# A routed feed-forward on one core: 71 blocks instead of 72, and the last batch finished in two halves

## The chip, the cores and the metric

The kernel runs on one core of a Trainium2 chip. The metric is the device time of one execution in microseconds (us); less is better. Before the change the median of three runs is 690.12 us.

## The reference

One layer of a transformer on x of shape (8, 512, 128), that is 8 batches of 512 rows, all in float32:

```
x = layernorm(x + attention(x))          # 16 heads of 8
gates = sigmoid(x @ Wg)                  # 8 experts, the best 2 of each row, weights normalised to 1
shared = silu(x @ Ws1) * (x @ Ws3) @ Ws2
routed = sum over the 2 experts e of w_e * (silu(x @ We1[e]) * (x @ We3[e])) @ We2[e]
out = layernorm(x + (shared + routed) / 3)
```

## The kernel before, in words

The kernel has an attention part (up to about 530 us) and a feed-forward part. Each of the five engines runs its own hand-written order of instructions; semaphores (`need`, `wait_ge`, `then_inc`) join them.

**Blocks.** While attention runs, each row of x is scattered twice into `slots_dram`, once for each expert it chose, so that every block of 128 slots belongs to one expert. 4096 rows times 2 give 8192 entries, 64 full blocks; each of 8 experts can leave a block open, so the kernel computes `SLOTS` = 72 blocks, in `G` = 9 groups k of `NBUF` = 8 (r = 0 to 7). Slots that no row fills hold a blank row whose result is dropped.

**One block.** For block n = 8k + r, SP loads the 128 slots (`moe_sync.block`, L1270). TensorE turns them (L1559), multiplies them with the expert's first weights in three products (L1579 to L1581), turns the gated result (L1589) and multiplies with the second weights (L1601). ScalarE applies silu (L1470) and scales the result (L1477); VectorE multiplies (L1418) and copies (L1414). GpSimd scatters the 128 results with an indirect DMA to `y2_dram` (L1242), where each row of x has two places. The engines take one block after another in `run_blocks`, which runs G + 4 = 13 groups; in the last four no blocks are left, and `exists` skips their steps.

**The end of a batch.** Blocks of group k hold rows of batches up to k, so batch n is complete when group n + 1 has been scattered. `ended(g, 3)` is the batch whose pairs SP loads at the end of group k (`load_pairs`, L1259: 512 KB, two rows of results for each row of x) after it has waited for the scatters (`y_stored`). VectorE then adds the pair (`add_pair`, L1363), adds the shared part and x (`add_sum`, L1370), takes statistics (`final_statistics`, L1376) and aggregates them (`final_mean`, L1384), for each of the four tiles of 128 rows, and forms variance and negated mean of all four (L1388, L1389). In steady work these steps are spread over the blocks of a group. One group later (`ended(g, 4)`) GpSimd raises the variance to the power -1/2 and multiplies (`final_deviation`, L1227 and L1229, at r = 0 ahead of the group's scatters), ScalarE normalises four tiles (`final_normalize`, L1452) and issues the store of 256 KB to the output (`store_out`, L1457).

**Order at the end.** In GpSimd's program the deviation of batch 5 stands after the scatters of group 8 (blocks 64 to 71), followed by those of batches 6 and 7. The sums z have two buffers, so batch 7 may be added only when batch 5's store has landed:

```
if c == 0:
    need(dve, yb_loaded[slot], 16 * (uses + 1))
    need(dve, out_stored[slot], 16 * uses)
```

VectorE's last rows take batch 7 tile by tile; in these lists `prob` is the large tile in which all buffers of this part lie.

Of the kernel before, what the change touches and what calls it, by code (L numbers as in the profile page):

```python
# [41 lines left out]
ALU = mybir.AluOpType  # L42
# [3 lines left out]
P = 128  # L46
EPS = 1e-5
TOP_K = 2
# [62 lines left out]
def layer(nc, x, w_qkv, b_qkv, w_out, b_out, wg, ws1, ws3, ws2, we1, we3, we2, out):  # L111
    B, S, D = x.shape
    E, _, F = we1.shape
    NC = 16
    HD = D // NC
    NCH = S // P
    QUADS = B * S // P
    TILES = QUADS
# [9 lines left out]
    ROW = D + 2  # L128
    NFC = F // P
    NBUF = 8  # L130
    assert SLOTS % NBUF == 0 and SLOTS % 8 == 0
    jobs = Jobs(B)
    SETUP_STEPS = 4
    CLEARS = 7
# [3 lines left out]
    with ctx:  # L138
# [6 lines left out]
        def sem(name):  # L145
            return ctx.enter_context(nc.semaphore(name))
# [983 lines left out]
        y_stored = [sem(f"y_stored{n}") for n in range(NBUF)]  # L1130

        yb_loaded = [sem(f"yb_loaded{r}") for r in range(2)]
        pair_done = sem("pair_done")
        z_done = sem("z_done")
        fstats_done = sem("fstats_done")
# [26 lines left out]
        AHEAD = 3  # L1162

        def vector_count(n, copied, multiplied, turned):

            return AHEAD + 3 * n - min(n, 2) - max(n - (SLOTS - AHEAD), 0) + (n >= 2 and copied) + multiplied \
                + (n < SLOTS - AHEAD and turned)

        def y_ebT_count(n):

# [1 line left out]

        def copied_count(n):

            return vector_count(n + 2, True, False, False) if n + 2 < SLOTS else \
                vector_count(SLOTS - 1, True, True, True) + n + 2 - (SLOTS - 1)

        def gated_count(n):

# [4 lines left out]
            return n + 1 if n < AHEAD else vector_count(n - AHEAD, True, True, True)  # L1184

        def exists(k, r, back=0):
            return not isinstance(k, int) or 0 <= NBUF * k + r - back < SLOTS


        hT = scoreA[:].rearrange("p a b x -> p (a b) x")  # L1190
# [20 lines left out]
        def moe_gpsimd(pool):  # L1211
            pool.wait_ge(pv_done, QUADS)
            pool.iota(block_no_i[:], pattern=[[0, 1]], base=0, channel_multiplier=1).then_inc(late_const, 1)
            pool.memset(turn[:], 1.0).then_inc(late_const, 1)
            pool.wait_ge(late_const, 2)
            pool.tensor_copy(block_no[:], block_no_i[:]).then_inc(late_const, 1)
            pool.memset(turn[:, :, E - 1:E], float(1 - E)).then_inc(late_const, 1)
            deviation(pool, B)
            scatter_rows(pool, B - 2, range(NCH * TOP_K))
            copy_rows(pool, B - 1)  # L1220
            scatter_rows(pool, B - 1, range(NCH * TOP_K))

            def final_deviation(n):

                need(pool, fve_done, 2 * (n + 1))
                need(pool, norm_done, 4 * n)
                pool.tensor_tensor(frs[:], fve[:], half[:], ALU.pow).then_inc(frs_done, 1)  # L1227
                need(pool, frs_done, n + 1)
                pool.tensor_tensor(fmr[:], fneg[:], frs[:], ALU.mult).then_inc(fmr_done, 1)  # L1229

            def block(g, r):
                k = g.k
                n = NBUF * k + r
                if r == 0 and ended(g, 4):
                    final_deviation(ended(g, 4).n)
                if not exists(k, r):
                    return

                at = NBUF * g.odd + r
                need(pool, block_loaded[at], 16 * (g.m + 1))  # L1240
                need(pool, y_done, n + 1)
                pool.indirect_dma_start(y2_dram, bass.IndirectOffsetOnAxis(ap=eb[:, at, D:D + 1].bitcast(I32), axis=0),  # L1242
                                        yo[:, r, :], None, bounds_check=TOP_K * TILES * P, oob_is_err=False) \
                    .then_inc(y_stored[r], 16)

            run_blocks(pool, block)

        def moe_sync(sp):

            store_x1(sp, B)  # L1250
            sp.wait_ge(x1_stored, 64 * B)
            load_x1(sp, B - 1)

            sp.wait_ge(scattered, CLEARED + 16 * TILES * TOP_K)

            def load_pairs(batch):

                need(sp, pair_done, 4 * (batch.n - 1))
                sp.dma_start(yb[:, batch.slot].rearrange("p c j d -> p (c j d)"),  # L1259
                             y2_rows[batch.n] if isinstance(batch.n, int) else  # L1260
                             y2_rows[bass.ds(batch.n, 1)].rearrange("b p x -> (b p) x")).then_inc(yb_loaded[batch.slot], 16)
# [12 lines left out]

            run_blocks(sp, block)
            for slot in range(2):
                sp.wait_ge(out_stored[slot], 16 * (B // 2))

        def moe_vector(dve):
            def beside(n):  # L1280
# [97 lines left out]
            def final_mean(batch, c):  # L1378
# [5 lines left out]
                dve.bn_aggr(fmv[:, c, :], fst[:, c, :]).then_inc(fmv_done, 1)  # L1384
                if c == 3:
                    dve.wait_ge(fmv_done, 4 * n + 4)
                    need(dve, fmr_done, n)
                    dve.tensor_scalar(fve[:], fmv[:, :, 1], EPS, None, ALU.add).then_inc(fve_done, 1)  # L1388
                    dve.tensor_scalar(fneg[:], fmv[:, :, 0], -1.0, None, ALU.mult).then_inc(fve_done, 1)  # L1389

            def beside_block(g, r):
                before_last, this = ended(g, 4), ended(g, 3)
# [30 lines left out]

            run_blocks(dve, block)

        def moe_scalar(act):
            for n in range(STEPS):
                b, c = n // 4, n % 4
# [17 lines left out]
            for n in range(3):  # L1446
                ebT_round(n, n)

            def final_normalize(batch, c):
                need(act, fmr_done, batch.n + 1)  # L1450
# [12 lines left out]
            def block(g, r):  # L1463
                k = g.k
                n = NBUF * k + r
                if exists(k, r):
                    act.wait_ge(h_gT_ready, n + 1)
                    if n >= 2:
                        act.wait_ge(vector_done, gated_count(n - 2))
                    act.activation(silu[:, r % 2, :], h_bank(r)[:, 0:F], ACT.Silu).then_inc(silu_done, 1)  # L1470
                if exists(k, r, 4):
                    c = (r - 4) % NBUF
                    at = NBUF * ((g.odd + (r - 4) // NBUF) % 2) + c
                    act.wait_ge(y_ebT_ready, y_ebT_count(n))
# [6 lines left out]
                if ended(g, 4):  # L1481
                    for c in NORMALIZED_AT.get(r, ()):
                        final_normalize(ended(g, 4), c)
                    if r == NBUF - 1:
                        store_out(ended(g, 4))

            run_blocks(act, block)

        def moe_tensor(pe):

# [76 lines left out]
            def block(g, r):  # L1567
# [23 lines left out]
                if n < SLOTS + 2:  # L1591
# [68 lines left out]
```

## Time and profile before

| | |
|---|---|
| median of three runs | 690.12 us (687.95 to 690.82) |
| the profiled execution, its own time | 686.2 us |
| its span | 684.5 us |
| TensorE (PE) busy | 640.4 us, 94% |
| VectorE (DVE) busy | 548.9 us, 80% |
| ScalarE (ACT) busy | 424.2 us, 62% |
| GpSimd (POOL) busy | 269.4 us, 39% |
| mean granted TensorE clock | 0.98 of full speed |

The span runs from the first to the last instruction of the profile; the execution's own time is 1.7 us longer. The profile names lines of the kernel and tiles; PE is TensorE's matmuls, PEld its weight loads, SPq and ACTq are the queues on which SP and ScalarE issue DMAs. Idle time of an engine matters only if the engine is on the chain of work that ends last.

### The profile page before, as it was taken

The numbers are of one execution on the slowest core, as the hardware profiler recorded it, in microseconds if no ns is written. First come the engines' busy times: TensorE is split into PE (matmuls) and PEld (weight loads), VectorE is DVE, ScalarE is ACT, GpSimd is POOL, SyncE is SP. The second block draws the span as 40 slices with busy tenths as digits, with TensorE's granted clock in tenths as the row PEclk, the third lists the DMA queues.
The fourth block names the chain that finished last, engine by engine and source line by source line (L and its number), as shares of the span: only waits on it lengthen the run. The fifth ranks groups of instructions, "written<-read, shape, count | busy, mean of one in ns | idle before, by whom it ended". The sixth has DMA issues, their size and how long they took to land.

```text
span 684.5 us, 16202 instructions
## 1 busy us (share of the span) xinstructions
PE 640.4 (94%) x4653; PEld 320.8 (47%) x4653; DVE 548.9 (80%) x1272; ACT 424.2 (62%) x973; POOL 269.4 (39%) x402
## 2 busy tenths in 40 slices
PE   8899999999999999999999999999899989999970
PEld 5442333333334333333343334333258878888760
DVE  4895677779897997998899799797667767888882
ACT  2065677776676776677767667766734346666752
POOL 3322112333144335314434432540525526677772
PEclk9998899999999999999999999999999999999995
DMA  4557466344433324442333342330132033444522
GB/s 84 122 122 175 100 137 156 82 88 105 74 84 79 84 50 78 96 89 62 85 72 64 89 101 53 66 89 15 52 108 63 32 83 88 146 141 132 164 74 77
DMA packets 161857, 62.68 MB, mean 92 GB/s; under 512 B 110586, under 2 KB 155516, under 8 KB 161808
## 3 DMA queue, kind: packets, MB, share of 16 engines
q1 hardware_dynamic: 155008, 46.72, 31.2%
q0 software_dynamic: 5648, 13.26, 6.4%
q10 hardware_dynamic: 1152, 2.10, 0.8%
q8 instruction: 24, 0.39, 0.2%
q14 instruction: 25, 0.20, 0.1%
HBM read 38.04 MB, written 24.26 MB: 91 GB/s over the span
## 4 chain that ended last, share of the span: by engine, by line
PE 64%; issue 11%; POOL 8%; DVE 7%; DMA 4%; ACT 4%; SPq 2%; POOLq 0%; ACTq 0%; DVEq 0%
PE pvp L1051 16%; PE scoreB L1026 15%; PE scoreA L1012 14%; POOL y_dram L1242 6%; DVE mx L946 4%; DMA parts_dram<-parts 3%; ACT prob L919 2%; PE shared L534 2%; PE scoreB L1527 2%; PE shared L523 2%; PE pvp L995 1%; PE shared L518 1%; PE shared L553 1%; POOL prob L1227 1%; PE shared L542 1%
## 5 line engine op out<-in xcount | busy, mean ns | idle before, releaser
L919 ACT ACTIVATE prob<-scoreB 128x512 f32<-128x512 f32 x512 | 278.7, 600 | 125.9 <-PE scoreB L1026 125.5
L946 DVE TENSOR_REDUCE mx<-scoreA 128x2 f32<-128x1024 f32 x256 | 304.5, 1219 | 65.1 <-PE scoreA L1012 62.5
L1026 PE MATMUL scoreB<-qs,ks 74*128 74x512 bf16 x512 | 197.0, 387 | 6.4 <-ACT prob L919 3.0
L1012 PE MATMUL scoreA<-ks,qs 72*128 72x512 bf16 x512 | 195.2, 386 | 4.7 <-DMA ks<-parts_dram 2.4
L1051 PE MATMUL pvp<-prob,v 128*32 128x512 f32 x1024 | 137.6, 611 | 0.8 <-ACT pv_sb L911 0.8
L1012 PEld LDWEIGHTS scoreA<-ks,qs 72*128 72x128 bf16 x512 | 49.6, 99 | 138.9 <-DVE mx L946 65.1
L1026 PEld LDWEIGHTS scoreB<-qs,ks 74*128 74x128 bf16 x512 | 49.3, 97 | 100.3 <-ACT prob L919 77.6
L1242 POOL DMA_INDIRECT y_dram<-prob x72 | 70.8, 983 | 44.2 <-issue 30.7
L497 POOL DMA_INDIRECT slots_dram<-rows,slot_i x64 | 63.3, 990 | 56.5 <-DMA ks<-parts_dram 31.4
L846 POOL CAST parts<-qk 128x256 bf16<-128x256 f32 x32 | 12.7, 396 | 180.9 <-ACT v_raw L572 169.6
L1601 PE MATMUL scoreB<-w,prob 128*128 x288 | 44.2, 276 | 1.1 <-DVE prob L1414 1.1
L1470 ACT ACTIVATE prob<-scoreA 128x256 f32<-128x256 f32 x72 | 27.6, 383 | 22.4 <-PE pvp L1589 10.7
L1601 PEld LDWEIGHTS scoreB<-w,prob 128*128 128x128 f32 x288 | 37.8, 191 | 1.5 <-issue 1.3
L1579 PE MATMUL scoreA<-w_high,ebT_high 128*128 x72 | 34.5, 480 | 3.5 <-DVE gated L1418 3.5
L1418 DVE TENSOR_TENSOR gated<-scoreA,prob 128x256 f32<-128x256 f32 x72 | 30.2, 420 | 7.9 <-ACT prob L1470 7.4
L1051 PEld LDWEIGHTS pvp<-prob,v 128*32 128x32 f32 x1024 | 20.4, 108 | 29.4 <-issue 27.8
L1477 ACT ACTIVATE prob<-scoreB,prob 128x128 f32<-128x128 f32 x72 | 26.6, 369 | 11.7 <-PE scoreA L1559 9.3
L568 ACT ACTIVATE qk<-shared,bq 128x128 f32<-128x128 f32 x64 | 20.0, 363 | 18.7 <-PE shared L523 11.1
L645 POOL TENSOR_SCALAR veps<-mv 128x4 f32<-128x4 f32 x8 | 1.8, 227 | 73.2 <-DVE mv L627 73.2
L1348 DVE TENSOR_TENSOR ebT_low<-scoreA,ebT_high 128x128 fp32r<-128x128 f32 x72 | 20.8, 290 | 10.4 <-ACT ebT_high L1444 8.6
L1581 PE MATMUL scoreA<-w_high,ebT_low 128*128 x72 | 28.4, 395 | 0.0
L1580 PE MATMUL scoreA<-w_low,ebT_high 128*128 x72 | 28.3, 394 | 0.0
(178 smaller groups left out, 921.0 us busy)
## 6 DMA issues: line engine op xcount, KB each, us to landing
qs<-parts_dram SPq DMA_DIRECT2D x96, 96.0 KB
parts_dram<-parts SPq DMA_DIRECT2D x32, 192.0 KB
slots_dram<-blank POOLq DMA_DIRECT2D x9, 520.0 KB, 7.2
prob<-slots_dram SPq DMA_DIRECT2D x72, 65.0 KB, 1.9
ks<-parts_dram SPq DMA_DIRECT2D x64, 64.0 KB
prob<-y_dram SPq DMA_DIRECT2D x8, 512.0 KB, 3.3
ks<-parts_dram SPq DMA_DIRECT2D x32, 96.0 KB
xin<-in_L_attn_x SPq DMA_DIRECT2D x32, 64.0 KB, 2.2
```

Source lines behind the costliest of these rows:

```text
L497: pool.indirect_dma_start(slots_dram, bass.IndirectOffsetOnAxis(ap=slot_i[:, j, t:t + 1], axis=0), rows[:, t, j, :], None).then_inc(scatte ...
L919: act.activation(prob[:, i % 2, j, 2 * u + c, :], scoreB[:, c], ACT.Exp, scale=SCALE).then_inc(exp_done, 1)
L946: dve.tensor_reduce(mx[:, i % 2, at // 2, at % 2 * 2:at % 2 * 2 + 2], scoreA[:, at % 2], AX.X, ALU.max).then_inc(max_done, 1)
L1012: ins = pe.matmul(scoreA[:, at % 2, c], qs[0:KR, st, j, qc * P:(qc + 1) * P], ks[0:KR, st, j, :], start=True, stop=True)
L1026: pe.matmul(scoreB[:, c], ks[0:KM, i, j, kc * P:(kc + 1) * P], qs[0:KM, i, j, :], start=True, stop=True).then_inc(b_ready, 1)
L1051: ins = pe.matmul(pvp[32 * h:32 * h + 32, :], v[:, (i - 1) % 2, h, j, :], prob[:, (i - 1) % 2, h, j, :], start=(j == 0), stop=(j == 3))
L1242: pool.indirect_dma_start(y2_dram, bass.IndirectOffsetOnAxis(ap=eb[:, at, D:D + 1].bitcast(I32), axis=0), yo[:, r, :], None, bounds_check= ...
L1418: dve.tensor_tensor(gated[:, r % 4, :], h_bank(r)[:, F:2 * F], silu[:, r % 2, :], ALU.mult) \
L1579: pe.matmul(h, ebT_highs[:, r % 4], high, start=True, stop=False)
L1580: pe.matmul(h, ebT_highs[:, r % 4], low, start=False, stop=False)
L1581: ins = pe.matmul(h, ebT_lows[:, r % 4], high, start=False, stop=True)
L1601: ins = pe.matmul(y_bank(r), gatedT[:, (r - 4) % 4, c * P:(c + 1) * P], w2_flat[:, bass.ds(e * NFC * D + c * D, D)], start=(c == 0), stop= ...
```

## The change

The number of blocks that are computed becomes 71: eight experts with a remainder of at least one row each leave at most (8192 + 8 x 127) / 128 = 71.9, so that 71 blocks hold every row. `SLOTS`, 72, stays the size of the slots' memory and of its clearing. The counts that the engines wait for are formed with `BLOCKS`.

The last batch (7) is taken out of the loop over groups on VectorE, GpSimd and ScalarE and stands behind it in two halves of two tiles: each half has its own load, its own variance, power, normalisation and store (128 KB). Within a half VectorE takes each operation for both tiles before the next.

```diff
+    BLOCKS = (TILES * P * TOP_K + E * (P - 1)) // P
...
+        last_half_loaded = sem("last_half_loaded")
...
         def exists(k, r, back=0):
-            return not isinstance(k, int) or 0 <= NBUF * k + r - back < SLOTS
+            return not isinstance(k, int) or 0 <= NBUF * k + r - back < BLOCKS
...
-            def final_deviation(n):
-
-                need(pool, fve_done, 2 * (n + 1))
+            def final_deviation(n, tiles, count):
+
+                lo, hi = tiles[0], tiles[-1] + 1
+                need(pool, fve_done, 2 * count)
                 need(pool, norm_done, 4 * n)
-                pool.tensor_tensor(frs[:], fve[:], half[:], ALU.pow).then_inc(frs_done, 1)
-                need(pool, frs_done, n + 1)
-                pool.tensor_tensor(fmr[:], fneg[:], frs[:], ALU.mult).then_inc(fmr_done, 1)
+                pool.tensor_tensor(frs[:, lo:hi], fve[:, lo:hi], half[:, lo:hi], ALU.pow).then_inc(frs_done, 1)
+                need(pool, frs_done, count)
+                pool.tensor_tensor(fmr[:, lo:hi], fneg[:, lo:hi], frs[:, lo:hi], ALU.mult).then_inc(fmr_done, 1)
...
             run_blocks(pool, block)
+            for h in range(2):
+                final_deviation(B - 1, range(2 * h, 2 * h + 2), B + h)
...
+                to = yb[:, batch.slot].rearrange("p c j d -> p (c j d)")
+                width = NCH * TOP_K * D if batch.n < B - 1 else NCH * TOP_K * D // 2
+                for at in range(0, NCH * TOP_K * D, width):
+                    sp.dma_start(to[:, at:at + width], y2_rows[batch.n][:, at:at + width]) \
+                      .then_inc(yb_loaded[batch.slot] if at == 0 else last_half_loaded, 16)
...
-                    need(sp, y_stored[r], 16 * (k - 1))
+                    need(sp, y_stored[r], 16 * min(k - 1, (BLOCKS - r + NBUF - 1) // NBUF))
...
             run_blocks(dve, block)
 
+            last = Batch(B - 1, (B - 1) % 2, (B - 1) // 2)
+            for h in range(2):
+                tiles = range(2 * h, 2 * h + 2)
+                if h == 1:
+                    dve.wait_ge(last_half_loaded, 16)
+                for c in tiles:
+                    add_pair(last, c)
+                for c in tiles:
+                    add_sum(last, c)
+                for c in tiles:
+                    final_statistics(last, c)
+                for c in tiles:
+                    final_aggregate(last, c)
+                variance_and_mean(B - 1, tiles)
...
             run_blocks(act, block)
+
+            last = Batch(B - 1, (B - 1) % 2, (B - 1) // 2)
+            for h in range(2):
+                for c in range(2 * h, 2 * h + 2):
+                    final_normalize(last, c, B + h)
+                act.wait_ge(norm_done, 4 * (B - 1) + 2 * h + 2)
+                act.dma_start(out_rows[B - 1][:, 2 * h * D:2 * (h + 1) * D],
+                              z[:, last.slot, 2 * h:2 * h + 2].rearrange("p c d -> p (c d)")) \
+                   .then_inc(out_stored[last.slot], 16)
```

`final_aggregate` and `variance_and_mean` are the two parts of the former `final_mean`.

GpSimd's program at its end, from block 70 on, in the kernel before (L1242 is the scatter of a block's results, L1227 the power, L1229 the product):

```order
L1242 DMA y2_dram<-prob 8193x128 [waits y_done,block_loaded6]
L1242 DMA y2_dram<-prob 8193x128 [waits y_done,block_loaded7]
L1227 TENSOR_TENSOR prob<-prob,half 128x4 [waits norm_done,fve_done]
L1229 TENSOR_TENSOR prob<-prob 128x4 [waits frs_done]
L1227 TENSOR_TENSOR prob<-prob,half 128x4 [waits norm_done,fve_done]
L1229 TENSOR_TENSOR prob<-prob 128x4 [waits frs_done]
L1227 TENSOR_TENSOR prob<-prob,half 128x4 [waits norm_done,fve_done]
L1229 TENSOR_TENSOR prob<-prob 128x4 [waits frs_done]
```

and in the changed kernel, where the same three lines are numbered L1245, L1230 and L1232:

```order
L1245 DMA y2_dram<-prob 8193x128 [waits y_done,block_loaded6]
L1230 TENSOR_TENSOR prob<-prob,half 128x4 [waits norm_done,fve_done]
L1232 TENSOR_TENSOR prob<-prob 128x4 [waits frs_done]
L1230 TENSOR_TENSOR prob<-prob,half 128x4 [waits norm_done,fve_done]
L1232 TENSOR_TENSOR prob<-prob 128x4 [waits frs_done]
L1230 TENSOR_TENSOR prob<-prob,half 128x2 [waits norm_done,fve_done]
L1232 TENSOR_TENSOR prob<-prob 128x2 [waits frs_done]
L1230 TENSOR_TENSOR prob<-prob,half 128x2 [waits norm_done,fve_done]
L1232 TENSOR_TENSOR prob<-prob 128x2 [waits frs_done]
```

One scatter is gone from between block 70's and batch 5's power, and batch 7's power and product are there twice, on two columns each.

VectorE's program for batch 7 in the kernel before, from its first pair (L1363) on; the rows of the other tiles repeat these:

```order
L1363 TENSOR_TENSOR prob<-prob 128x128 [waits out_stored1,yb_loaded1]
L1370 TENSOR_TENSOR prob<-prob 128x128 [waits pair_done]
L1363 TENSOR_TENSOR prob<-prob 128x128
L1370 TENSOR_TENSOR prob<-prob 128x128 [waits pair_done]
...
L1376 BN_STATS prob<-prob 128x6 [waits z_done]
L1384 BN_AGGR prob<-prob 128x2 [waits fstats_done]
...
L1388 TENSOR_SCALAR prob<-prob 128x4 [waits fmr_done,fmv_done]
L1389 TENSOR_SCALAR prob<-prob 128x4
```

and in the changed kernel (the pair is L1370, the sum L1377, the statistics L1383, the aggregate L1399, variance and negated mean L1390 and L1391), the first half and the beginning of the second:

```order
L1370 TENSOR_TENSOR prob<-prob 128x128 [waits out_stored1,yb_loaded1]
L1370 TENSOR_TENSOR prob<-prob 128x128
L1377 TENSOR_TENSOR prob<-prob 128x128 [waits pair_done] x2
L1383 BN_STATS prob<-prob 128x6 [waits z_done] x2
L1399 BN_AGGR prob<-prob 128x2 [waits fstats_done,fve_done]
L1399 BN_AGGR prob<-prob 128x2 [waits fstats_done]
L1390 TENSOR_SCALAR prob<-prob 128x2 [waits fmr_done,fmv_done]
L1391 TENSOR_SCALAR prob<-prob 128x2
L1370 TENSOR_TENSOR prob<-prob 128x128 [waits last_half_loaded]
L1370 TENSOR_TENSOR prob<-prob 128x128
```

Before, each sum follows the pair that it waits for and each aggregate its own statistics; now an operation of the other tile stands between them, and the variance of two tiles stands ahead of the other two tiles' pairs.

## Rows read from the trace of the kernel before

**Rows 1.** The page, part 4: the chain that ended last, shares by line.

```profile
PE pvp L1051 16%; PE scoreB L1026 15%; PE scoreA L1012 14%; POOL y_dram L1242 6%; DVE mx L946 4%; DMA parts_dram<-parts 3%; ACT prob L919 2%; PE shared L534 2%; PE scoreB L1527 2%; PE shared L523 2%; PE pvp L995 1%; PE shared L518 1%; PE shared L553 1%; POOL prob L1227 1%; PE shared L542 1%
```

**Rows 2.** Stretches: length; PE, PEld, DVE, ACT, POOL busy; PEclk; DMA share; GB/s.

```profile
660.00:670.00 10.00, 3.90 (x29) 3.28 (x27) 6.60 (x29) 2.98 (x9) 8.02 (x9) 0.84 0.20 69
670.00:684.50 14.50, 0.00 (x0) 0.00 (x0) 4.24 (x20) 4.94 (x12) 2.42 (x5) 0.50 0.24 90
```

**Rows 3.** The chain in order of time, from 660 us: start, length, what.

```profile
667.69 0.97 POOL y_dram L1242
...
668.67 1.06 POOL prob L1227
...
671.72 2.24 DMA out<-prob
...
674.06 0.30 DVE prob L1363
...
678.92 1.02 POOL prob L1227
...
680.24 1.65 ACT prob L1452 x4
```

**Rows 4.** SP's load of batch 7; landing times of L1259 from 640 us on.

```profile
669.94 0.32 SPq L1259 DMA_DIRECT2D prob<-y_dram  x1
...
prob<-y_dram SPq DMA_DIRECT2D x1, 512.0 KB, 3.2
...
DMA to landing us min/median/max: 3.2/3.3/3.7
```

**Rows 5.** The timeline of GpSimd from 655 us: start, length, engine, line.

```profile
656.81 1.06 POOL L1227 TENSOR_TENSOR prob<-prob,half 128x4 f32<-128x4 f32 x1
658.72 1.03 POOL L1242 DMA_INDIRECT y_dram<-prob  x1 [0.57 <-issue]
...
666.42 0.97 POOL L1242 DMA_INDIRECT y_dram<-prob  x1 [0.30 <-issue]
```

**Rows 6.** The timeline of ScalarE: block 70 scaled, the last store's issue.

```profile
663.23 0.37 ACT L1477 ACTIVATE prob<-scoreB,prob 128x128 f32<-128x128 f32 x1 [0.26 <-PE scoreB L1601]
...
681.92 0.34 ACTq L1457 DMA_DIRECT2D out<-prob  x1
```

**Rows 7.** The timeline of VectorE in batch 7's part.

```profile
675.97 0.29 DVE L1370 TENSOR_TENSOR prob<-prob 128x128 f32<-128x128 f32 x1
676.18 0.29 DVE L1376 BATCH_NORM_STATS2 prob<-prob 128x6 f32<-128x128 f32 x1
676.64 0.18 DVE L1384 BATCH_NORM_AGGREGATE prob<-prob 128x2 f32<-128x6 f32 x1 [0.17 <-DVE prob L1376]
676.78 0.29 DVE L1376 BATCH_NORM_STATS2 prob<-prob 128x6 f32<-128x128 f32 x1
...
678.38 0.18 DVE L1384 BATCH_NORM_AGGREGATE prob<-prob 128x2 f32<-128x6 f32 x1
678.60 0.17 DVE L1388 TENSOR_SCALAR prob<-prob 128x4 f32<-128x4 f32 x1
678.68 0.16 DVE L1389 TENSOR_SCALAR prob<-prob 128x4 f32<-128x4 f32 x1
```

**Rows 8.** Groups of GpSimd's instructions over the span: count, busy us, mean ns.

```profile
L1227 POOL TENSOR_TENSOR prob<-prob,half 128x4 f32<-128x4 f32 x8 | 8.7, 1089 | 7.7 <-DVE prob L1389 5.8 <-ACT prob L1452 1.8
L490 POOL TENSOR_SCALAR ids_i<-ids_i 128x8 int32<-128x8 int32 x8 | 2.0, 245 | 1.3 <-POOL rows L488 1.0
L645 POOL TENSOR_SCALAR veps<-mv 128x4 f32<-128x4 f32 x8 | 1.8, 227 | 73.2 <-DVE mv L627 73.2
L1229 POOL TENSOR_TENSOR prob<-prob 128x4 f32<-128x4 f32 x8 | 1.6, 200 | 0.6
```

**Rows 9.** DMA from 681 to 684.5 us, in 40 slices, and the last store.

```profile
DMA  0000000000000000000079999998200000000000
...
out<-prob ACTq DMA_DIRECT2D x1, 256.0 KB, 2.0
```

More of the change, by code:

```diff
@@ L130, in layer @@
     NBUF = 8
-    assert SLOTS % NBUF == 0 and SLOTS % 8 == 0
+    BLOCKS = (TILES * P * TOP_K + E * (P - 1)) // P
+    assert SLOTS % NBUF == 0 and SLOTS % 8 == 0 and SLOTS - NBUF < BLOCKS <= SLOTS
     jobs = Jobs(B)
@@ L1164, in vector_count @@
         def vector_count(n, copied, multiplied, turned):
-            return AHEAD + 3 * n - min(n, 2) - max(n - (SLOTS - AHEAD), 0) + (n >= 2 and copied) + multiplied \
-                + (n < SLOTS - AHEAD and turned)
+            return AHEAD + 3 * n - min(n, 2) - max(n - (BLOCKS - AHEAD), 0) + (n >= 2 and copied) + multiplied \
+                + (n < BLOCKS - AHEAD and turned)
         def y_ebT_count(n):
@@ L1173, in copied_count @@
         def copied_count(n):
-            return vector_count(n + 2, True, False, False) if n + 2 < SLOTS else \
-                vector_count(SLOTS - 1, True, True, True) + n + 2 - (SLOTS - 1)
+            return vector_count(n + 2, True, False, False) if n + 2 < BLOCKS else \
+                vector_count(BLOCKS - 1, True, True, True) + n + 2 - (BLOCKS - 1)
         def gated_count(n):
@@ L1233, in block @@
                 n = NBUF * k + r
-                if r == 0 and ended(g, 4):
-                    final_deviation(ended(g, 4).n)
+                if r == 0 and ended(g, 4) and ended(g, 4).n < B - 1:
+                    final_deviation(ended(g, 4).n, range(NCH), ended(g, 4).n + 1)
                 if not exists(k, r):
@@ L1258, in load_pairs @@
                 need(sp, pair_done, 4 * (batch.n - 1))
-                sp.dma_start(yb[:, batch.slot].rearrange("p c j d -> p (c j d)"),
-                             y2_rows[batch.n] if isinstance(batch.n, int) else
-                             y2_rows[bass.ds(batch.n, 1)].rearrange("b p x -> (b p) x")).then_inc(yb_loaded[batch.slot], 16)
+                to = yb[:, batch.slot].rearrange("p c j d -> p (c j d)")
[3 more added lines that the diff above has]
+                      .then_inc(yb_loaded[batch.slot] if at == 0 else last_half_loaded, 16)
             def block(g, r):
@@ L1275, in moe_sync @@
             run_blocks(sp, block)
-            for slot in range(2):
-                sp.wait_ge(out_stored[slot], 16 * (B // 2))
+            sp.wait_ge(out_stored[0], 16 * (B // 2))
+            sp.wait_ge(out_stored[1], 16 * (B // 2 + 1))
         def moe_vector(dve):
@@ L1376, in final_statistics, with variance_and_mean, final_aggregate @@
                 dve.bn_stats(fst[:, c, :], z[:, batch.slot, c, :]).then_inc(fstats_done, 1)
-            def final_mean(batch, c):
+            def variance_and_mean(n, tiles):
+                lo, hi = tiles[0], tiles[-1] + 1
+                dve.wait_ge(fmv_done, 4 * n + hi)
+                need(dve, fmr_done, n)
+                dve.tensor_scalar(fve[:, lo:hi], fmv[:, lo:hi, 1], EPS, None, ALU.add).then_inc(fve_done, 1)
+                dve.tensor_scalar(fneg[:, lo:hi], fmv[:, lo:hi, 0], -1.0, None, ALU.mult).then_inc(fve_done, 1)
+            def final_aggregate(batch, c):
                 n = batch.n
@@ L1384, in final_mean @@
                 dve.bn_aggr(fmv[:, c, :], fst[:, c, :]).then_inc(fmv_done, 1)
+            def final_mean(batch, c):
+                final_aggregate(batch, c)
                 if c == 3:
[L1386 to L1389, printed above, removed]
+                    variance_and_mean(batch.n, range(NCH))
             def beside_block(g, r):
-                before_last, this = ended(g, 4), ended(g, 3)
+                before_last, this = (batch if batch and batch.n < B - 1 else None for batch in (ended(g, 4), ended(g, 3)))
                 if r == 0 and before_last:
@@ L1447, in moe_scalar, with final_normalize @@
                 ebT_round(n, n)
-            def final_normalize(batch, c):
-                need(act, fmr_done, batch.n + 1)
+            def final_normalize(batch, c, count):
+                act.wait_ge(fmr_done, count)
                 at = z[:, batch.slot, c, :]
@@ L1480, in block @@
                     ebT_round(r + 3, n + 3)
-                if ended(g, 4):
+                if ended(g, 4) and ended(g, 4).n < B - 1:
                     for c in NORMALIZED_AT.get(r, ()):
-                        final_normalize(ended(g, 4), c)
+                        final_normalize(ended(g, 4), c, ended(g, 4).n + 1)
                     if r == NBUF - 1:
@@ L1590, in block @@
                                            gated[:, (r - 2) % 4, c * P:(c + 1) * P], ident[:])
-                if n < SLOTS + 2:
+                if n < BLOCKS + 2:
                     ins.then_inc(h_gT_ready, 1)
```

## The prediction

> **What bounds the kernel now.** The first view is the chain that ended last over the whole span: matmuls of the attention part carry most of it [rows 1], and no line the change touches stands among them except the scatter of block results (L1242, 6%) and the normalisation's power (L1227, 1%). So the change can act at the end only, and the stretches of the end come next [rows 2]: TensorE is busy 3.9 of the 10 us from 660 to 670, and not at all in the last 14.5 us. The granted clock there falls to 0.50 (the 1.2 GHz level), which costs nothing, as no matmul follows.
>
> The chain of the last 25 us, in order of time, says what ends last [rows 3]. The last scatter (block 71) starts at 667.69; GpSimd then takes up batch 5's power (668.67), ScalarE normalises batch 5, its store is issued at 671.72 and lands 2.24 later; only then may VectorE start batch 7 (674.06), because batches 5 and 7 share a buffer of z. Batch 7 then goes serially through VectorE, GpSimd (678.92), ScalarE (680.24) and one store. The reader is to see that batch 7 waits for batch 5's **store**, not for its own rows: their load is issued at 669.94 and lands 3.2 later, at 673.1, some 0.8 before the store does at 673.96 [rows 4].
>
> Why GpSimd comes to batch 5 so late is seen in its own instructions [rows 5]. After batch 4's power it starts block 64 at 658.72 and goes on every 1.27 us, 0.97 busy and 0.30 idle, to block 71. It does not wait for results: ScalarE had scaled block 70 by 663.60 [rows 6], while GpSimd reached it at 666.42. It is 2.8 us late, and each scatter is worth its whole 1.27 on the chain.
>
> **The change, part by part.** I count against the profiled execution (span 684.5, time 686.2; 0.6% below the median of 690.12) and carry the difference over to the median. About 0.5%, 3.45 us, is what a measurement of this kernel can tell from no change.
>
> *Block 71 is left out.* GpSimd loses one scatter. Block 70's then ends at 667.39 and batch 5's power follows: 668.67 becomes 667.40, **-1.27 us**, and batch 5's normalisation, its store and batch 6's part come earlier with it. The rest that leaves with block 71 is worth nothing: its load (65 KB), its matmuls and transposes on TensorE, and what VectorE and ScalarE do for it stood ahead of its scatter, under a GpSimd that was behind. If that cover were gone (block 70's result late by over 2.8 us), the gain of 1.27 would shrink by the excess. VectorE copies block 70 ahead of its wait for batch 4's store, so that wait holds nothing that GpSimd needs. SP's load of batch 7 waits for the last scatter in either kernel, so it too is issued 1.27 earlier, near 668.7.
>
> *VectorE in two parts.* Today it takes 4.62 us from the first pair (674.06) to the negated means (678.68) of four tiles, with each operation waiting for the one before [rows 7]. For two tiles in the new order I use the gaps of those rows: 0.21 to the next independent operation (675.97 to 676.18), 0.46 from statistics to their own aggregate, 0.14 between aggregates, 0.22 from the last aggregate to the variance, 0.08 to the negated mean. Pairs at 0 and 0.21, sums at 0.42 and 0.63, statistics at 0.84 and 1.05, aggregates at 1.30 and 1.51, variance at 1.73, negated mean at 1.81; the second half begins near 1.95 and has its negated mean at 3.76. That is 0.86 sooner than 4.62, because the interleaving fills the waits; the two extra small operations are in it.
>
> *GpSimd and ScalarE in two parts.* The first half's power starts 0.24 after its negated mean, at 2.05, and its product ends at 3.34; the second half asks for GpSimd at 4.00, so the added power and product (1.3 us) are hidden by VectorE's second half. ScalarE normalises two tiles from 3.37 to 4.25 and issues the added store (0.34) by 4.62, before it is wanted again at 5.32; nothing of the second half queues behind it. From power to first normalisation is 1.32 today (678.92 to 680.24), so the second half runs from 5.32; four normalisations take 1.65 today, two take about 0.88, and its store is issued at 6.23 against 7.86 (681.92 less 674.06). That is -1.63; I take **-1.6**, with 1.3 as the other end, for the semaphore steps between statistics, which the new order may repeat.
>
> *The power on two columns* has no row. The same operation on four takes 1.02 to 1.06 us at the end [rows 3], and a product of the same four columns 0.20 [rows 8], so 0.82 is the power itself. If that is by column, two columns take 0.6 (-0.4); if it is fixed, 1.02 (0). A loss is excluded, since it is the same operation on half the elements. No row is nearer to one end, so I take **-0.2**. GpSimd's simpler operations hardly mind the width: 0.245 on eight columns, 0.227 on four [rows 8]; if the power were like them, the term would be 0. The Trainium skill's page "GPSIMD Engine Reference" (section 3.1, Elementwise — side-by-side cycle accounting) counts about 2.6 cycles for an element beside a dispatch for each instruction, which speaks against cutting the work in two: by it the sum would be 3.2. The simple rows agree with that rule; no row here shows it for the power.
>
> *The last store* is 128 KB instead of 256. Alone, 256 KB takes 2.0 to land, and the DMA engines move it in some 0.8 of these: nine of forty slices of 3.5 us [rows 9]. Half the bytes save at most 0.4, and nothing if rows of 1 KB instead of 2 KB take as long each; I take **-0.3**. The first half's store is moving two us earlier and is out of the way.
>
> *The load in two pieces* costs SP one issue more (0.32) with only the last waits behind it. The first piece is half as large and has the slack of 0.8 above; the second is not wanted until 1.95 after VectorE's start. Nothing, by these.
>
> The sum: 1.27 + 1.6 + 0.2 + 0.3 = 3.37, **3.4 us**, from 2.6 (1.27 + 1.3) to 3.7 (1.27 + 1.63 + 0.4 + 0.4). On the median that is 690.12 - 3.4 = 686.7, 0.49% down: just inside what counts as no change.
>
> **The rivals.** (a) *The end above 3.45*: the power goes by column, and the store halves. For it: 0.82 of 1.02 is not the fixed part of a GpSimd instruction. The time is 686.4. (b) *The power's cost is fixed*, like that of the simple operations: 3.2, 686.9. For it: 18 ns for four columns more. This is the page's rule as a mechanism of this kernel. Forecast, (a) and (b) are one mechanism with other sizes, and the line of 0.5% runs through them. (c) *The scatter was not the bound*: something else releases batch 5 at 668.67, and only the tail's 2.1 remains, 688.0. Against it speak the 2.8 us by which GpSimd trails ScalarE. (d) *The second piece of the load becomes a wait of its own*: on SP's queue it lands behind the first. Issued near 669.0, it decides from 674.7 on (VectorE at 672.8, and 1.95); at twice the 3.2 of the whole load it would land at 675.4, and the gain shrinks by 0.7, to 687.4. (e) *Slower*: the same wait, grown by contention with batch 5's store. The gain is gone if the piece lands after 678.1, 9 us after its issue, and the kernel is slower by 0.5% only if it lands after 681.5; the loads seen here take 3.2 to 3.7 [rows 4]. Time from 693.6. (f) *The change doesn't do what it says*: a block more or less on the chain would show as no change, 690.1; yet GpSimd's order does lose one scatter.
>
> **How the numbers follow.** The forecast has 0.38, (a) 0.27, (b) 0.18, (c) 0.05, (d) 0.06, (e) 0.02, (f) 0.04. The runs of before spread by 2.9 us (687.95 to 690.82), almost as much as the gain, so that medians can well stand 1 us to either side of the sum; the sum lies 0.05 from the line. Beyond 0.5% I therefore put 0.19 of the forecast, 0.20 of (a) and 0.06 of (b): 0.45. Slower is 0.03, from (e) and the spread about (f). The rest, 0.52, is no change. Forecast: 686.7, within 0.5%. The range runs from the larger sum with 1.4 of the spread, 685.0, to rival (c) with 0.6, 688.6; the sum with its own bounds alone is 686.4 to 687.5.
>
> **What would show it.** Right: GpSimd's last scatter stands some 14.7 us before the end (16.8 today) and is followed at once by batch 5's power; VectorE's first pair of batch 7 is still released by a store; from that pair to the last issue of a store about 6.2 (power 0.8) instead of 7.86; the last store lands in about 1.7. Wrong: a wait of VectorE in the middle of batch 7 (d, e); idle time of GpSimd before batch 5's power (c); a power on two columns at 1.0 or 0.6, which would move the sum to 3.2 or 3.6; or stretches before 655 us that differ between the two kernels by more than 1 us, on which the change has no hold.

## The result, and the profile after

The changed kernel takes 684.03 us (median of 22 runs, 680.78 to 690.05), the kernel before 687.95 (22 runs, 682.99 to 692.62). The ratio of the runs is 0.9948, with a 95% interval of 0.9923 to 0.9973 (the two medians alone give 0.9943): 0.52% less, clear of no change. The forecast gain of 0.49% lies well inside that interval. Two things were nevertheless wrong. The time, 684.03, lies below the range of 685.0 to 688.6; and the forecast said "within 0.5%", where the kernel became faster, by a hair beyond that line; the interval holds the line itself, 0.995, so that the runs do not tell on which side of it the kernel stands.

First the chain of the profiled execution of the changed kernel, which answers to [rows 3]; start, length, what (L1245 is the scatter, L1230 the power, L1370 the pair, L1482 the normalisation):

```profile
667.45 0.97 POOL y_dram L1245
668.42 1.08 POOL prob L1230
...
671.48 2.36 DMA out<-prob
...
673.94 0.49 DVE prob L1370 x2
...
677.80 0.71 POOL prob L1230
...
678.81 0.88 ACT prob L1482 x2
```

The order of the chain is the old one: last scatter, batch 5's power, its store, VectorE, GpSimd, ScalarE, a store. The clock times hide the gain of the scatter, since in this execution everything ahead of the end lies later: block 64's scatter starts at 659.62 and not at 658.72 as in [rows 5]. Counted from there to the end of the span, the kernel before takes 25.78 us (684.50 less 658.72) and the changed one 22.38 (682.00 less 659.62). **This stretch, 3.40 us shorter, is the measure of all that follows**; it leaves out what happens ahead of the change.

The timeline of the last batch in the changed kernel, which answers to [rows 6, 7]:

```profile
659.62 1.03 POOL L1245 DMA_INDIRECT y_dram<-prob  x1 [0.57 <-issue]
...
673.94 0.49 DVE L1370 TENSOR_TENSOR prob<-prob 128x128 f32<-128x128 f32 x2 [3.82 <-DMA out<-prob]
...
675.72 0.16 DVE L1391 TENSOR_SCALAR prob<-prob 128x2 f32<-128x2 f32 x1
675.79 0.48 DVE L1370 TENSOR_TENSOR prob<-prob 128x128 f32<-128x128 f32 x2
675.96 0.87 POOL L1230 TENSOR_TENSOR prob<-prob,half 128x2 f32<-128x2 f32 x1 [3.08 <-DVE prob L1391]
...
677.56 0.16 DVE L1391 TENSOR_SCALAR prob<-prob 128x2 f32<-128x2 f32 x1
677.80 0.70 POOL L1230 TENSOR_TENSOR prob<-prob,half 128x2 f32<-128x2 f32 x1 [0.69 <-DVE prob L1391]
678.05 0.34 ACTq L1524 DMA_DIRECT2D out<-prob  x1
...
678.81 0.88 ACT L1482 ACTIVATE prob<-prob 128x128 f32<-128x128 f32 x2 [0.80 <-POOL prob L1232]
679.72 0.34 ACTq L1524 DMA_DIRECT2D out<-prob  x1
```

The first pair is still released by a store. The second half's first pair starts 0.07 after the start of the first half's negated mean, without a wait for its own load. GpSimd and ScalarE work on the first half beside VectorE's second, and the added store is issued (678.05) beside GpSimd's second power. The last store, 128 KB, takes 1.7 to land (256 KB: 2.0, [rows 9]):

```profile
out<-prob ACTq DMA_DIRECT2D x1, 128.0 KB, 1.7
```

### The profile page after: what moved, and what is told of

It reads as the page before. It is cut to its first block, busy times and chain, and to the rows that moved or that the text cites. A ratio compares the mean times of both kernels' runs of the same rounds, so it can differ in the third digit from the quotient of the medians.

```text
span 682.0 us, 16170 instructions
## 1 busy us (share of the span) xinstructions
PE 638.3 (94%) x4643; PEld 319.2 (47%) x4643; DVE 547.2 (80%) x1271; ACT 423.5 (62%) x970; POOL 270.3 (40%) x403
## 4 chain that ended last, share of the span: by engine, by line
PE 60%; issue 11%; POOL 10%; DVE 9%; DMA 4%; ACT 4%; SPq 1%; POOLq 0%; ACTq 0%; DVEq 0%
PE pvp L1052 17%; PE scoreB L1027 15%; PE scoreA L1013 13%; POOL y_dram L1245 7%; DVE mx L947 5%; DMA parts_dram<-parts 2%; ACT prob L920 2%; PE shared L535 2%; PE shared L524 1%; PE pvp L996 1%; DMA ks<-parts_dram 1%; PE shared L519 1%; POOL prob L1230 1%; PE shared L543 1%; PE shared L554 1%
## 5 line engine op out<-in xcount | busy, mean ns | idle before, releaser
L1027 PE MATMUL scoreB<-qs,ks 74*128 74x512 bf16 x512 | 195.0, 383 | 6.4 <-ACT prob L920 3.0
L1245 POOL DMA_INDIRECT y_dram<-prob x71 | 70.1, 987 | 43.8 <-issue 30.2
```

Source lines behind the costliest of these rows:

```text
L1027: pe.matmul(scoreB[:, c], ks[0:KM, i, j, kc * P:(kc + 1) * P], qs[0:KM, i, j, :], start=True, stop=True).then_inc(b_ready, 1)
```

## The experiments

Each kernel is read by the stretch from block 64's scatter to the end, and by its four pieces, in us: from that scatter to batch 5's power (the scatters), from there to VectorE's first pair of batch 7 (its release), from the pair to the last store's issue, and from that to the end. The runs of one kernel spread by 6 to 11 us, so that ratios tell differences of a few tenths of a per cent only roughly; the pieces come from one profile each, and equal code repeats in them within 0.1 to 0.4.

| kernel | sum | scatters | release | pair to issue | last store |
|---|---|---|---|---|---|
| before | 25.78 | 9.95 | 5.39 | 7.86 | 2.58 |
| changed | 22.38 | 8.80 | 5.52 | 5.78 | 2.28 |
| 71 blocks alone | 24.95 | 8.92 | 5.62 | 7.86 | 2.55 |
| halves alone | 23.46 | 9.96 | 5.45 | 5.78 | 2.27 |
| new order, not cut | 23.37 | 8.89 | 5.74 | 6.17 | 2.57 |
| third buffer | 20.78 | 8.70 | 4.08 | 5.79 | 2.21 |
| three tiles and one | 22.32 | 8.71 | 5.50 | 5.93 | 2.18 |
| third buffer, VectorE normalises | 20.08 | 8.71 | 3.95 | 5.15 | 2.27 |

**The two parts of the change, each alone.** The first kernel is the one before with 71 blocks, counted as in the change, and its old end. The second is the changed kernel with

```diff
-    BLOCKS = (TILES * P * TOP_K + E * (P - 1)) // P
+    BLOCKS = SLOTS
```

> The kernel before with 71 blocks and its old end in one part. Measure: from the start of block 64's scatter on GpSimd to the end of the span, 25.78 us before (684.50 less 658.72) and 22.38 in the changed kernel (682.00 less 659.62). Theory (GpSimd's scatters are serial and bound the release of batch 5): one scatter less, 24.5 to 24.6, that is 1.15 to 1.3 less than before; time 0.17% lower. Rival (something else releases batch 5, the scatter was covered): 25.8. In both, the start of block 64 itself may stand anywhere from 657 to 661, since nothing ahead of it differs.

> The changed kernel with 72 blocks, so the halves alone. Theory (the parts add up, since they lie one behind the other on the chain): 22.38 + 1.2 = 23.5 to 23.7 from block 64's scatter to the end. Rival (the halves pay only where the scatter is gone, since the load of batch 7 is issued after the last scatter and its second piece would bind): above 24.2, with a wait of VectorE in the middle of batch 7.

71 blocks alone: 24.95, a gain of 0.83, a miss, as 1.15 to 1.3 were expected; ratio 0.9988 (0.9956 to 1.0019). The scatters' piece is 1.03 shorter, so GpSimd's chain does bound and the rival falls; 0.23 was lost in the release, where batch 5's store took 2.48 to land and not 2.24 as before. Of the 1.27, one scatter's pace, the profiles with 71 blocks show 1.03 to 1.25; in the changed kernel's, one scatter takes 1.07 instead of 0.97. The halves alone: 23.46, just below the lower edge of what was expected, without a wait between the halves; ratio 0.9979 (0.9944 to 1.0015). Neither ratio is clear of no change; it is the profiles that show the two gains. The gains of 0.83 and 2.32 add up to 3.15, beside 3.40 for both together. That fits parts that lie one behind the other, within the 0.1 to 0.4 to which the pieces repeat.

**The order of operations without the cut.** All four tiles in the new order on VectorE, one variance, one power, one store; the load stays in two pieces.

```diff
-            for h in range(2):
-                tiles = range(2 * h, 2 * h + 2)
+            for tiles in (range(NCH),):
...
-            for h in range(2):
-                final_deviation(B - 1, range(2 * h, 2 * h + 2), B + h)
+            final_deviation(B - 1, range(NCH), B)
...
+            for c in range(NCH):
+                final_normalize(last, c, B)
+            store_out(last)
```

> 71 blocks, all four tiles of the last batch in the new order of operations, but one variance, one power on four columns, four normalisations and one store of 256 KB; the load stays in two pieces. Theory (the order on VectorE gives about 1.3, halving the work behind it 0.8, the smaller store 0.3): VectorE's part from first pair to negated mean 3.2 to 3.4 (4.62 before, 3.62 changed), first pair to store issue 6.5 (7.86 before, 5.78 changed), block 64 to the end 23.3 to 23.5. Rival (the cut in two gives it all, the order nothing): VectorE's part 4.5, block 64 to the end 24.4 or more.

The timeline of VectorE's part in this kernel (L1369 pairs, L1390 negated means):

```profile
672.16 0.90 DVE L1369 TENSOR_TENSOR prob<-prob 128x128 f32<-128x128 f32 x4 [4.05 <-DMA out<-prob]
672.97 0.89 DVE L1376 TENSOR_TENSOR prob<-prob 128x128 f32<-128x128 f32 x4
673.78 0.87 DVE L1382 BATCH_NORM_STATS2 prob<-prob 128x6 f32<-128x128 f32 x4
674.57 0.41 DVE L1398 BATCH_NORM_AGGREGATE prob<-prob 128x2 f32<-128x6 f32 x4
675.01 0.17 DVE L1389 TENSOR_SCALAR prob<-prob 128x4 f32<-128x4 f32 x1
675.09 0.16 DVE L1390 TENSOR_SCALAR prob<-prob 128x4 f32<-128x4 f32 x1
```

From the pair to the negated mean it takes 2.93 us: 4.62 before, 3.62 in two halves. The new order alone takes 1.69 off VectorE's part, more than the 1.3 expected. Cutting in two gives 0.69 of it back there, as each half has its own waits and its own variance (from aggregates to variance 0.39 and 0.42 instead of 0.44 once), and takes 1.08 off behind it, so that from pair to issue only 0.39 is left of the cut (6.17 against 5.78), and 0.29 on the store. The ratio, 0.9953 (0.9922 to 0.9984), is not to be told from the changed kernel's. That the sum, 23.37, lies in the expected range is luck: VectorE's part was shorter than expected, and batch 5's store, landing in 2.59, made the release 0.35 longer than before.

**Does batch 7 wait for batch 5's store?** The changed kernel with a third buffer of z for the last batch (`z_of` is 2 for it):

```diff
-                    need(dve, out_stored[slot], 16 * uses)
+                    if n < B - 1:
+                        need(dve, out_stored[slot], 16 * uses)
```

> The changed kernel, with a third buffer of z for the last batch, so that it does not wait for batch 5's store. Theory (batch 7 waits for that store and its own rows are there before): VectorE's first pair is released by the load's first piece, 2.8 us after its issue, some 1.0 to 1.4 earlier against block 64; block 64 to the end 21.0 to 21.4. Rival (the rows land with the store or after it, or GpSimd's and ScalarE's work for batch 6 is in the way): 22.2 to 22.4, no gain.

The chain of this kernel:

```profile
662.94 2.12 DMA y_dram<-prob
665.26 2.72 DMA prob<-y_dram
668.00 0.51 DVE prob L1374 x2
```

Now the last scatter and the first piece of the load release VectorE, and the release is 1.44 shorter. So in the changed kernel it was the store, and the load comes next; for the kernel before, [rows 3] say the same, and no run takes the store away there. The stretch is 20.78, somewhat better than the 21.0 to 21.4 expected, since the scatters' piece and the last store were 0.1 shorter as well. The ratio, 0.9952 (0.9923 to 0.9981), hides it in the spread of the runs.

**What does the power cost by column?** Parts of three tiles and one:

```diff
-            for h in range(2):
-                tiles = range(2 * h, 2 * h + 2)
+            for tiles in (range(3), range(3, 4)):
...
-            for h in range(2):
-                final_deviation(B - 1, range(2 * h, 2 * h + 2), B + h)
+            for h, tiles in enumerate((range(3), range(3, 4))):
+                final_deviation(B - 1, tiles, B + h)
```

> The last batch in parts of three tiles and one. It measures the power on three columns and on one. By column (0.155 each beside 0.39 fixed, from 1.01 on four and 0.70 on two): 0.86 and 0.55. Rival (fixed, and the 0.70 only the absence of VectorE beside it): 0.7 or more on one column. First pair to last store issue about 6.0, since ScalarE's three tiles are in the way of the fourth; block 64 to the end 22.4 to 22.7, no better than two and two.

GpSimd's timeline of this kernel:

```profile
678.86 0.85 POOL L1230 TENSOR_TENSOR prob<-prob,half 128x3 f32<-128x3 f32 x1 [3.62 <-DVE prob L1391]
679.79 0.19 POOL L1232 TENSOR_TENSOR prob<-prob 128x3 f32<-128x3 f32 x1
680.39 0.55 POOL L1230 TENSOR_TENSOR prob<-prob,half 128x1 f32<-128x1 f32 x1 [0.41 <-DVE prob L1391]
681.02 0.19 POOL L1232 TENSOR_TENSOR prob<-prob 128x1 f32<-128x1 f32 x1
```

0.55, 0.70, 0.85 and 1.01 us for one to four columns: about 0.15 for a column beside 0.4 that is fixed. The product stays at 0.19 to 0.20. Three and one end no sooner than two and two (22.32 and 22.38; pair to issue 5.93 and 5.78): the fourth tile has to wait for ScalarE, as expected. Its product ends at 681.21, and ScalarE, after three tiles and the added store's issue, takes it up at 681.69.

**Shortening the last steps.** Third buffer, and the second half normalised by VectorE from mean and power, without the product:

```diff
+                dve.tensor_scalar(at, at, fmv[:, c, 0:1], frs[:, c:c + 1], ALU.subtract, ALU.mult).then_inc(last_done, 1)
...
+                    act.wait_ge(last_done, 2)
```

> Third buffer of z, and the second half's two tiles normalised by VectorE, straight from mean and power, without GpSimd's product and without ScalarE. Theory (the last steps are serial, each takes its time off the end): product 0.28 and the second of two normalisations 0.3 go, the store is issued 0.5 to 0.7 sooner; block 64 to the end 20.1 to 20.3 against 20.78. Rival (a wait on two engines' semaphores and VectorE's start take it back): 20.7.

20.08, 0.70 less than with the third buffer alone, as expected. A second profile of the same kernel (below) has 20.26.

**The level of the runs.** The profiles show block 64 starting anywhere from 655.2 to 662.4 us, although all kernels of the table have the same work ahead of it. One thing that differs is the granted clock in two places. The stretches of the kernel before, and of 71 blocks alone, from 58 us (stretch, length, then busy time of PE, PEld, DVE, ACT, POOL, the granted clock, DMA share, GB/s):

```profile
58.00:60.00 2.00, 2.00 (x46) 0.86 (x45) 1.41 (x2) 1.77 (x6) 0.40 (x1) 1.00 0.70 193
60.00:62.00 2.00, 0.60 (x8) 0.00 (x0) 0.65 (x1) 1.06 (x2) 1.81 (x4) 1.00 0.53 112
62.00:64.00 2.00, 1.82 (x6) 0.77 (x7) 0.79 (x1) 0.96 (x2) 1.17 (x2) 0.68 0.92 270
64.00:68.00 4.00, 4.00 (x15) 0.74 (x13) 2.12 (x4) 1.43 (x3) 0.00 (x0) 0.50 1.18 259
68.00:72.00 4.00, 4.00 (x15) 1.77 (x17) 2.65 (x3) 2.39 (x4) 0.00 (x0) 0.50 0.49 58
72.00:74.00 2.00, 2.00 (x12) 0.36 (x5) 0.35 (x2) 0.07 (x1) 0.00 (x0) 0.76 0.69 201
```

```profile
60.00:62.00 2.00, 1.04 (x9) 0.13 (x9) 1.04 (x1) 1.46 (x3) 1.77 (x4) 1.00 0.69 107
62.00:64.00 2.00, 1.97 (x9) 0.69 (x9) 1.18 (x2) 1.40 (x3) 1.57 (x3) 1.00 0.94 328
64.00:68.00 4.00, 3.97 (x26) 1.41 (x28) 3.61 (x6) 2.93 (x6) 0.00 (x0) 1.00 1.31 221
68.00:72.00 4.00, 4.00 (x26) 1.03 (x19) 3.20 (x5) 2.23 (x5) 0.00 (x0) 1.00 0.37 58
```

In the first, TensorE waited for a load (0.60 busy of 2 us), and the clock then fell to 0.50, the 1.2 GHz level, for some ten us; there TensorE is busy throughout with 15 matmuls in 4 us instead of 26. In the second the same wait was shorter, and the clock stayed. The waits of the two:

```profile
62.18 0.39 PE L1012 MATMUL scoreA<-ks,qs 72*128 72x512 bf16 x1 [1.58 <-DMA ks<-parts_dram]
```

```profile
61.95 0.39 PE L1013 MATMUL scoreA<-ks,qs 72*128 72x512 bf16 x1 [0.96 <-DMA ks<-parts_dram]
```

In the table's eight profiles this wait is 1.58 to 2.14 us in the four with the fall and 0.63 to 1.31 in the four without: here the fall goes with how late a load lands. The second place is the end of the attention part, in the changed kernel:

```profile
492.00:494.00 2.00, 1.50 (x11) 1.17 (x11) 0.56 (x1) 1.91 (x4) 0.80 (x1) 1.00 0.23 73
494.00:496.00 2.00, 1.93 (x9) 0.20 (x8) 1.16 (x4) 0.20 (x2) 1.52 (x4) 0.51 0.02 4
496.00:498.00 2.00, 1.26 (x8) 0.23 (x8) 0.00 (x0) 0.59 (x1) 1.30 (x2) 0.50 0.37 114
498.00:500.00 2.00, 2.00 (x12) 0.92 (x12) 0.25 (x1) 0.00 (x0) 0.00 (x0) 0.50 0.98 330
500.00:502.00 2.00, 2.00 (x16) 0.58 (x12) 1.72 (x10) 0.09 (x1) 0.00 (x0) 0.78 1.02 383
```

Of the eight kernels in the table, one profile shows no fall (block 64 at 656.75), four one fall (655.2 to 659.6), three both (661.1 to 662.4). As one with a fall starts sooner than the one without, the falls are not all of it.

What a fall costs can be read at the second place, where TensorE's waits are alike with a fall and without (0.47 for ScalarE, then 0.8). From VectorE's last two maxima of the scores to the first scatter of block results the kernels do the same work, but for the extra matmuls. The rows of 71 blocks alone, of the changed kernel, and of the first kernel with the extra matmuls described below:

```profile
466.19 2.59 DVE L947 TENSOR_REDUCE mx<-scoreA 128x2 f32<-128x1024 f32 x2 [0.25 <-PE scoreA L1013]
557.29 1.00 POOL L1243 DMA_INDIRECT y_dram<-prob  x1 [12.96 <-ACT prob L1478]
```

```profile
466.10 2.59 DVE L947 TENSOR_REDUCE mx<-scoreA 128x2 f32<-128x1024 f32 x2 [0.24 <-PE scoreA L1013]
560.09 1.00 POOL L1245 DMA_INDIRECT y_dram<-prob  x1 [12.94 <-ACT prob L1507]
```

```profile
466.42 2.59 DVE L947 TENSOR_REDUCE mx<-scoreA 128x2 f32<-128x1024 f32 x2 [0.25 <-PE scoreA L1023]
558.37 1.00 POOL L1257 DMA_INDIRECT y_dram<-prob  x1 [12.82 <-ACT prob L1519]
```

That is 91.10, 93.99 and 91.95 us. Over all twelve profiles it is 91.0 to 91.1 without a fall there (three), 92.7 to 94.0 with one (six), and 91.9 to 92.0 with extra matmuls and no fall (three): a fall takes 1.6 to 3.0 us, and the extra matmuls, with which none fell here, take 0.9 each time. At the first place, from VectorE's 29th maximum (near 55 us) to its 101st (near 187) the table's profiles take 133.9 to 134.6 us with the fall and 129.5 to 132.1 without.

Over 79 runs of the kernel before (one of 2112.16 us is left out), the span goes with its mean granted clock at a correlation of -0.86, 0.63 us for each 0.001. Two experiments put extra matmuls, whose results are not used, where TensorE waits, into the changed kernel and into the one with the third buffer:

```diff
+                if isinstance(b, int) and q == 2:
+                    keep(2, 3 * P, 8 * (q + 2) - 1)
+                if isinstance(b, int) and q == QUADS:
+                    keep(1, 3 * P, 8 * QUADS)
...
+                    if isinstance(b, int) and q == QUADS - 1:
+                        keep(1, P, 8 * QUADS)
```

> The changed kernel with extra matmuls, whose results are not used, where TensorE waits in the attention part: two at the stage that starts near 60 us (TensorE idle 1.3 to 1.6 there), one in each of the eight steps of the last scores, from 476 us, and one ahead of the last stage's products near 495. Theory (the level of the runs is set by whether the granted clock falls to 0.50 for some 5 to 10 us behind these waits, and the falls come after TensorE's idle time): no stretch below 1.00 at 60 to 76 and 486 to 506 us in the profile, mean granted clock over the runs from 0.983 to 0.986 or more, at 0.5 us of span for each 0.001 some 1.5 to 2.5 us less than the changed kernel, and a narrower spread of the runs. Rival (the falls have nothing to do with idle time): mean clock 0.983 as before, spread as before, time as the changed kernel's or up to 1 us more for the added matmuls. The tail from block 64 stays at 22.4 in both.

> The extra matmuls and the third buffer of z together. Theory: both gains add, 0.7% to 1.1% below the kernel before; block 64 to the end 20.8. Rival: as the third buffer alone, 0.5% below.

Neither profile shows a fall at the two places (the second shows one in the first 20 us), and the stretches are 22.22 and 21.00. The ratios are 0.9964 (0.9929 to 1.0000) and 0.9929 (0.9899 to 0.9959). But the mean clock over twelve runs is 0.984 in the first and 0.988 in the second, beside 0.982 for the kernel before in the runs taken with them: the first is a miss, and its runs spread by 8.6 us, no less than those of the kernel before. So the last two kernels had third buffer and normalisation by VectorE, with the matmuls and without:

> Third buffer, the second half normalised by VectorE, and the extra matmuls in the attention part. Theory on the tail: block 64 to the end 20.0 to 20.3, that is 5.6 less than before, with or without the extra matmuls. Theory on the level (the extra matmuls spare falls of the granted clock): mean clock over the runs at least 0.987, as in the second of the two kernels that had them (0.988) and not as in the first (0.984); 1.0% to 1.3% below the kernel before. Rival (the 0.988 was chance): mean clock 0.983, 0.7% to 0.9% below before.

> The same without the extra matmuls. Theory: block 64 to the end 20.0 to 20.3, mean clock 0.983 as in the changed kernel, 0.7% to 0.9% below before; the difference to the kernel with the matmuls is what they give. Rival (the clock is chance and the matmuls give nothing): both kernels within 0.2% of each other.

With: 0.9919 (0.9887 to 0.9950), mean clock 0.988. Without: 0.9929 (0.9895 to 0.9963), mean clock 0.985. The stretch is 20.30 and 20.26. The clock with the matmuls stands as the theory has it, but the times do not: 1.0% to 1.3% less were expected with them, and the two kernels lie 0.1% apart, as the rival has it. The profiles say why the gain is small at best: at the second place the matmuls take 0.9 us each time and can spare 1.6 to 3.0 only where the clock would have fallen. How often it falls there in the runs was not recorded, so what they give in the mean stays open. Both are faster than the kernel before by 0.7% to 0.8%, about twice their uncertainty, and by their stretch 2.1 us shorter than the changed kernel.

## Why the prediction was right and wrong

The mechanism held, and the sum with it: 3.37 forecast, 3.40 in the profiles, 0.49% forecast, 0.52% in the runs. That the sums agree to 0.03 is in part luck, as terms that are off by 0.11 to 0.14 in either direction cancel. Step by step:

| step | forecast | profiles |
|---|---|---|
| one scatter less | -1.27 | -1.15 |
| release of batch 7 | 0 | +0.13 |
| VectorE in two halves, pair to negated mean | -0.86 | -1.00 (4.62 to 3.62) |
| two normalisations instead of four | -0.77 | -0.77 |
| power on two columns | -0.2 | -0.31 |
| last store | -0.3 | -0.30 |

*The scatter*: GpSimd bounded as argued; the term is one pace of 1.27 less the 0.1 of a slower scatter, and the store behind it landed 0.1 to 0.4 later in these profiles. Rival (c) falls with the experiment on 71 blocks, and (f) with the seven scatters from block 64 on, where there were eight. *The halves*: the gaps that were read from one tile's serial operations gave 3.76 for the second negated mean, 3.62 was measured (the 0.14 "between aggregates" is in [rows 7] the gap from an aggregate to the next tile's statistics; the sum does not use it). This term and the normalisations were taken together as -1.6, short of their 1.63, for semaphore steps that might repeat; the profiles show -1.77, so nothing was to be held back. *The load in two pieces*: no wait, so (d) and (e) fall; the slack was there as read, since with the third buffer the load is the next limit and lets VectorE start 1.4 sooner than the store.

*The power*: here neither end was right. It is by column for the larger part, 0.15 a column, with 0.4 fixed, so two columns save 0.31. Rival (b), the fixed cost, falls. Rival (a), an end above 3.45, stays undecided: 3.40 in the profiles is 0.05 short of it, which is less than the pieces repeat to. The Trainium skill's page "GPSIMD Engine Reference" (section 3.1, Elementwise — side-by-side cycle accounting) gives about 2.6 cycles an element for `tensor_tensor`, by which the width would hardly count. The trace agrees for the product (0.19 for one and for three columns) and not for the power (0.15 more for each column).

**The step that failed** is the carrying over: "I count against the profiled execution ... and carry the difference over to the median", that is to 690.12, the middle of three runs, with "medians can well stand 1 us to either side" and 1.4 us of spread below the sum. Three runs that spread by 2.9 us were taken for the spread of this kernel. Its 22 runs spread by 9.6, and their median is 687.95; in three later sets of the same kernel it is 686.57 (35 runs), 685.75 (23) and 686.71 (22). Two of the three runs were among the slower. The profiled execution, 686.2, pointed there; it was named "0.6% below the median" and not weighed. Of the 2.7 us between the forecast 686.7 and 684.03, the starting point makes 2.2; 687.95 less 3.4 is 684.6, 0.5 above what came. A part of what the level hangs on was in the page of before as well: its granted clock shows an 8 in the fourth and fifth of the forty slices, the fall behind 62 us, which the prediction passed over. In the profiles such a fall takes 1.6 to 3.0 us at the one place and some 2 to 5 at the other, as much as the change. The prediction's own sign for this, stretches ahead of 655 us that differ by more than 1 us, stood at 0.90 between its two profiles (the start of block 64), and at 7.2 among the eight of the table. What else moves the level was not found.

The second miss, "no change" against "faster", hangs on 0.02% at a line that the sum had at 0.05 us. With the terms as measured the sum is 3.40 of a line of 3.45; at 687.95 the line is 3.44. Its chance of 0.45 for "faster" was the fair statement; choosing a side was no more than the toss of a coin.

## What to carry to other kernels

A tail in which several engines work one after another is shortened by any of its steps, and reading the gaps between dependent operations from one tile predicts the interleaved order to a few tenths of a us. Look there for interleaving first: without any cut it gave 1.69 of VectorE's part, and the cut into halves paid only for what lies behind VectorE. In runs this is not told apart: both kernels stand at 0.995. A forecast of an absolute time needs the spread of the kernel's runs as much as the effect: where the granted clock falls in some executions, three runs do not give the level, and a stretch of the profile that begins behind the falls measures a change that the runs' medians hide.

## What the runs showed of the hardware

- GpSimd's power on 128 partitions takes 0.55, 0.70, 0.85 and 1.01 us for one to four columns; the first half's power, on two columns, took 0.87 in the profiles where GpSimd had been idle for 3 us, and 0.71 where for 1.8. Idle time alone is not the reason, as three columns after 3.6 us took 0.85 and four after 5.8 took 1.01, and VectorE worked beside the power in both cases; the cause stays open.
- The last stores landed in 1.6 us for 64 KB (three tiles and one), 1.7 for 128 and 2.0 for 256: most of the time does not go with the bytes. Batch 5's stores of 256 KB, beside the load of batch 7, took 2.24 to 2.59.
- The granted clock fell to 0.50 for 3 to 10 us in some executions and not in others, at the same two places of the same code, behind stretches in which TensorE had waited. At the first place the wait was longer wherever it fell (1.58 to 2.14 us against 0.63 to 1.31); at the second the waits were alike with a fall and without. In two profiles of kernels with extra matmuls it fell elsewhere, in the first 20 us, and in one of them again near 108 us. A fall at the second place took 1.6 to 3.0 us of the span.
